# A vision-transformer block on one core: weight splits moved, high parts moved, and matmul groups at the norms

## The reference

```
h   = layernorm_3840(patches of x and of its four shifts) * gamma + beta, @ W + b   # tokens
h   = concat(cls, h)
y   = layernorm(h)
q, k, v = y @ Wq.T + bq, y @ Wk.T + bk, y @ Wv.T + bv          # 12 heads of 16
h   = h + softmax(q k.T / 4 + mask) v @ Wo.T + bo
z   = layernorm(h)
g   = top-2 gates of softmax(z @ router)                        # 8 experts of 192
routed = sum_e g_e * ((silu(z @ Wg_e) * (z @ Wu_e)) @ Wd_e)
shared = (silu(z @ Ws_gate) * (z @ Ws_up)) @ Ws_down            # 768 hidden
a   = sigmoid(z @ sg_w + sg_b)
out = h + a * shared + (1 - a) * routed
```

## Time and profile before

| | |
|---|---|
| median of 3 runs | 176.16 us (175.26 to 177.87) |
| profiled execution | 175.75 us, of which the span is 173.9 |
| granted TensorE clock, mean | 0.938 of 2.4 GHz |
| PE busy | 139.3 us, 80% |
| DVE busy | 120.5 us, 69% |
| ACT busy | 91.0 us, 52% |
| POOL busy | 42.1 us, 24% |

### The profile page before, as it was taken

One profiled execution on the slowest core, in us unless ns is written; L12 is line 12 of the kernel. 1 busy time (PEld: TensorE's weight loads), 2 busy tenths in 40 slices (PEclk: granted clock), 3 DMA queues, 4 the chain that ended last, 5 costly groups with the idle time before them and its releaser, 6 DMA issues.

```text
span 173.9 us, 4192 instructions
## 1 busy us (share of the span) xinstructions
PE 139.3 (80%) x1673; PEld 111.0 (64%) x1673; DVE 120.5 (69%) x297; ACT 91.0 (52%) x198; POOL 42.1 (24%) x55
## 2 busy tenths in 40 slices
PE   0449999903399988769806999999899999999992
PEld 0218777802177977659704567888777778878782
DVE  6299854699899996994626479787596562542753
ACT  0588865941277924444265769445645534343340
POOL 0000010000000000000000035536846858668430
PEclk9999999995579999999995589999999999999998
DMA  5999997000000000004991000048300000000003
GB/s 160 386 368 364 327 263 305 0 0 0 0 0 0 4 4 4 4 4 135 402 410 53 0 0 4 0 113 331 123 0 4 0 0 4 4 0 0 4 0 105
DMA packets 7391, 16.89 MB, mean 97 GB/s; under 512 B 800, under 2 KB 3612, under 8 KB 7372
## 3 DMA queue, kind: packets, MB, share of 16 engines
q1 hardware_dynamic: 7012, 16.29, 26.9%
q10 hardware_dynamic: 360, 0.34, 0.7%
HBM read 16.15 MB, written 0.47 MB: 96 GB/s over the span
## 4 chain that ended last, share of the span: by engine, by line
PE 50%; DVE 24%; ACT 9%; issue 5%; DMA 5%; ACTq 3%; POOL 2%; SPq 1%; DVEq 0%; POOLq 0%
PE PS L566 19%; PE PS L594 10%; PE PS L403 5%; DMA stage<-in_f_d_dram 5%; DVE piece L959 3%; DVE xsq L1115 3%; DVE mx L1111 2%; PE PS L322 2%; PE PS L415 2%; DVE vhl L1256 2%; PE PS L343 2%; PE PS L345 2%; PE PS L346 2%; PE PS L309 2%; POOL vhl L850 1%
## 5 line engine op out<-in xcount | busy, mean ns | idle before, releaser
L859 POOL TENSOR_TENSOR kq<-vhl,kq 128x296 f16<-128x296 f32 x35 | 29.5, 843 | 96.3 <-ACT kq L811 96.1
L1256 DVE SCALAR_TENSOR_TENSOR vhl<-PS,vhl 128x296 f32<-128x296 f32 x36 | 16.8, 466 | 21.6 <-POOL vhl L850 12.1
L804 ACT ACTIVATE vhl<-PS 128x296 f32<-128x296 f32 x36 | 15.0, 416 | 27.5 <-PE PS L566 27.5
L811 ACT ACTIVATE kq<-vhl 128x296 f16<-128x296 f32 x36 | 16.0, 445 | 5.5 <-DVE vhl L1256 5.5
L375 PE MATMUL PS<-cst,hn 128*128 128x128 f32 x10 | 4.0, 401 | 13.4 <-DVE hn L1035 13.4
L850 POOL TENSOR_TENSOR vhl<-vhl,xs 128x296 f32<-128x296 f32 x14 | 12.6, 903 | 5.5 <-issue 4.8
L1245 DVE TENSOR_TENSOR vhl<-vhl,xs 64x296 f32<-64x296 f32 (+1 forms) x18 | 10.2, 566 | 2.8 <-ACT vhl L804 2.6
L566 PE MATMUL PS<-XAh,piece 128*128 128x296 f16 x48 | 11.1, 316 | 0.2 <-DVE vhl L1256 0.2
L375 PEld LDWEIGHTS PS<-cst,hn 128*128 128x128 f32 x10 | 2.0, 201 | 14.0 <-DVE hn L1035 14.0
L566 PE MATMUL PS<-XAh,slab 128*128 128x296 f16 x48 | 10.0, 290 | 0.9 <-DVE vhl L1256 0.9
L343 PE MATMUL PS<-whl,xhl 128*128 128x193 f16 (+1 forms) x40 | 10.5, 262 | 0.0
(11 more groups left out here) (215 smaller groups left out, 403.0 us busy)
## 6 DMA issues: line engine op xcount, KB each, us to landing
slab<-in_w_inner_dram SPq DMA_DIRECT2D x3, 960.0 KB, 9.5
xs<-gate_rows_dram SPq DMA_DIRECT2D x8, 296.0 KB, 5.8
xs<-in_x_inner_dram SPq DMA_DIRECT2D x3, 592.0 KB, 10.5
stage<-in_f_a_dram SPq DMA_DIRECT2D x2, 768.0 KB, 10.4
stage<-in_f_b_dram SPq DMA_DIRECT2D x2, 768.0 KB, 11.7
stage<-in_f_d_dram SPq DMA_DIRECT2D x2, 576.0 KB, 13.2
xhl<-in_f_a_dram SPq DMA_DIRECT2D x1, 768.0 KB, 8.4
xhl<-in_f_b_dram SPq DMA_DIRECT2D x1, 768.0 KB, 9.3
```

Source lines behind the costliest of these rows:

```text
L804: A(silu[:, i % 2, :], PS[:, 3 + 2 * (i % 2), 0:HALF], ACT.Silu, scale=1.0 / XW).then_inc(S["a_silu"], 1)
L811: A(ah[:, f % ABUF, half * HALF:(half + 1) * HALF], hf[:, i % 3, :], ACT.Copy).then_inc(S["a_ah"], 1)
L859: G.tensor_tensor(al[:, f % ABUF, cols], hf[:, i % 3, :], ah[:, f % ABUF, cols], ALU.subtract).then_inc(S["g_al"], 1)
L1256: V.scalar_tensor_tensor(out=hf[:, i % 3, :], in0=PS[:, 4 + 2 * (i % 2), 0:HALF], scalar=SH / XW, in1=src[:, i % 2, :], op0=ALU.mult, op1= ...
```

## The change

Three kinds of edit, in the order of the engines:

- TensorE gets groups of matmuls of 512 columns whose results nobody reads, into bank 1 (free once the sums of squares have been read) and bank 6 (free between the attention and the second block half). At the first norm: 8 after `v_stat` has reached 5, 6 after the first three `h1` tiles, 6 after `v_stat` 10 and 4 after `v_stat` 11 (the reciprocal of `rsqrt(1)`). At the second: 6 right behind `wo(4)`, 4 after the last `h2` tile, 4 after `v_stat` 20 and 3 after `v_stat` 21.
- ScalarE converts WAh, WB and WC behind `squares(3)`, ahead of the bias rows, `sqrows` and `csum`. The second piece's first two high parts leave the place ahead of `root(3)`; all six stand at the steps 2 to 7 of the feed-forward, one a step (before: two ahead of the root and four at steps 2 to 5).
- VectorE makes the three low parts of the query and key weights ahead of the mean of the patches' norm, no longer behind `normed(0, range(3))`.

```diff
@@ tensor, ahead of transposes(0, ...)
+            def keep_warm(bank, n):
+
+                for _ in range(n):
+                    mm(PS[:, bank, :], WAh[:, 0:P], WAh[:, 0:512], start=True, stop=True)
+
+            pe.wait_ge(S["a_aw"], 1)
+            for name, count, n in (("v_stat", 5, 8), ("v_h", TILES + 3, 6), ("v_stat", 10, 6), ("v_stat", 11, 4)):
+                pe.wait_ge(S[name], count)
+                keep_warm(1, n)
@@ tensor, behind the output projection
             wo(4)
 
+            keep_warm(6, 6)
+            for name, count, n in (("v_h", 3 * TILES, 4), ("v_stat", 20, 4), ("v_stat", 21, 3)):
+                pe.wait_ge(S[name], count)
+                keep_warm(6, n)
             transposes(1, (0, 1, 2), range(TILES))
@@ scalar, behind the pixels
             squares(3)
 
+            act.wait_ge(d_aw, 80)
+            A(WAh[:, :], awst[:, 0, :], ACT.Copy, scale=SW).then_inc(S["a_aw"], 1)
+            A(WB[:, :], awst[:, 1, :], ACT.Copy, scale=SW).then_inc(S["a_aw"], 1)
+            A(WC[:, :], awst[0:CROWS, 2, :], ACT.Copy, scale=SW).then_inc(S["a_aw"], 1)
+
             act.wait_ge(S["p_bw"], 1)
...
             A(sqrows[:, 0:N].rearrange("p (a n) -> p a n", a=2), PS[:, 6:8, 0:HALF], ACT.Copy).then_inc(S["a_sqr"], 1)
-            act.wait_ge(d_aw, 80)
-            A(WAh[:, :], awst[:, 0, :], ACT.Copy, scale=SW).then_inc(S["a_aw"], 1)
-            A(WB[:, :], awst[:, 1, :], ACT.Copy, scale=SW).then_inc(S["a_aw"], 1)
-            A(WC[:, :], awst[0:CROWS, 2, :], ACT.Copy, scale=SW).then_inc(S["a_aw"], 1)
             act.wait_ge(S["p_main"], 1)
@@ scalar, second norm
             ctx_high(3)
-            ffn_high(1, 0)
-            ffn_high(1, 1)
             root(3)
@@ scalar, feed-forward loop
                     act_high(i - 1)
-                if 2 <= i < 6:
-                    ffn_high(1, i)
+                if 2 <= i < 8:
+                    ffn_high(1, i - 2)
@@ vector, ahead of the statistics
+            for k in range(3):
+                attention_low(k, 0, VC)
+
             stat = [0]
@@ vector, first norm
             normed(0, range(3))
-            attention_low(0, 0, VC)
-            attention_low(1, 0, VC)
-            attention_low(2, 0, VC)
             variances(2)
```

## The result

The changed kernel takes 173.96 us in the median of 20 runs (172.46 to 176.25), the kernel before 176.38 on the same chip (175.13 to 178.21); the ratio is 0.986, 95% interval 0.983 to 0.990. It is faster by 1.4%, clear of the interval but less than the 2% that the prediction took as telling: 2.4 us won where 5.2 were forecast (171.0, range 169.8 to 173.2), and the time lies outside the range. The profiled execution took 173.96, a span of 172.2.

The account below looks back on a forecast made before the run. VectorE paces the projections and TensorE the last stage, so only start time at the two norms could be won: 1.48 + 0.51 + 3.05 + 0.24 - 0.33 = 4.95 off 175.75 gives 170.8, taken as 171.0, range 169.8 to 173.2.

Parts of the forecast that it names:

- Part 1: First norm: VectorE's three low parts moved ahead of the statistics fill its idle time; gain 1.48 us, bounds 0.8 and 1.48.
- the first norm's clock: Matmul groups keep full clock there; earlier products and two closed VectorE gaps in the projections gain 0.51 us, bounds 0 to 0.75.
- The conversions and `csum`: First norm, ScalarE: weight conversions push `csum` to 32.9 at worst, before VectorE asks at about 34.8; cost nothing.
- Part 2: Second norm: moving two high parts from ahead of the root brings the reciprocal earlier; gain 3.05 us, lower bound 1.77.
- the table load: Second norm, ScalarE: goes right behind the last context copy, some 2 us before the variances; 1.28 us if left behind the wait.
- The gate's wait: Feed-forward step 6: a high part ahead of the gates' copy makes TensorE stand 0.33 us, bounds 0 and 0.6.
- Part 3: Matmul groups in TensorE's pauses at both norms hold the clock: gains 0.51 and 0.24 us, bounds 0 and 0.75 for both.
- the second norm's clock: Groups there spare ScalarE's XAh its wait for cold transposes: gain 0.24 us.
- Rival (a): Clock falls all the same around the norms' transposes, losing 0.51 + 0.24 and up to 0.7: 171.8 to 172.5; chance 0.12.
- Rival (c): Groups at both norms run at half clock ahead of the transposes, 3.9 and 3.6 us late: 179.2; chance 0.05.
- Rival (b): Feed-forward gives back more: a second stall like the gate's, table load left behind its wait: 172.6; chance 0.10.

Follow-up runs that it names:

- e1: Changed kernel without any of the matmul groups, moved splits and high parts kept: 177.53 us, ratio to before 1.008.
- e8: Changed kernel with ten matmuls in the attention's pause but no groups at the two norms: 175.46 us, ratio to before 0.997.
- e2: Kernel before with the norms' matmul groups alone added: 177.71 us.
- e7: e3 with the second piece's last two high parts at steps 7 and 8, behind the gates' copy: 170.54 us, ratio to before 0.971.
- e3: Changed kernel with ten more matmuls of 512 columns in the attention's pause ahead of the fourth unit's transposes: 171.85 us, ratio to before 0.977.
- e5: e3 with the second piece's first two high parts put back ahead of the second norm's root: 174.81 us, ratio to before 0.995.
- e11: e5 without the attention's ten matmuls: 173.99 us, ratio to before 0.986.
- e4: e3 with four matmuls instead of ten in the attention's pause: four runs, 171.01, 171.43, 174.70 and 174.82 us.
- e6: e3 with the attention weights' splits put back on ScalarE and VectorE: 173.28 us, ratio to before 0.989.

## Why the prediction was wrong

**Part 1** was right as a sum with the first norm's clock: 1.48 + 0.51 = 1.99 forecast, 1.96 measured to the maxima (1.55 to XAl and 0.41 behind it, so that the agreement to 0.03 is in part luck: one of the two gaps that the 0.51 is made of stayed). As terms they don't stand alone: the moved splits without groups gave 0.40 and 0.49 (e1, e8), the groups without moved splits were 1.32 slower in the profile of e2 (35.11 for 33.79). The splits bring the second matmuls forward, and with the clock down (from about 37.5 to 51 in e1, 40.7 to 51 in e8) TensorE then gives most of that back; the groups held it where no pause of 3.4 us followed them. The conversions and `csum` cost nothing; the weights landed at 26.1.

**Part 2** was right at its place: 3.05 forecast, 3.05 in the profiles (4.04 to 0.99), the table load where it was said to go. The gate's wait, 0.33 forecast, is 0.36 (e7). But the 3.05 are a gain only where the attention is on time (e3 against e5, 3.0 in the runs); where it is late by as much they are 0 (the changed kernel against e11).

**Part 3**: no group delayed a transpose, the second norm's clock gave 0.51 instead of 0.24. The step that failed is one that the prediction did not cost: it gave the clock back at the two norms and put the attention between them at no change, without a reason; the profile of before showed 1.00 there, for one execution. Rival (a), a fall around the norms' transposes, had the mechanism, at another place than the one that cost the time; at its own place the fall came in one profile only (e7, 1.0 us). Its reason against, that no gap left is as long as those in which the clock fell before, is what the runs refute: the clock fell 0.8 us after a pause of 2.65 us, 0.2 after one of 1.69 (e4), and in the midst of small matmuls (e1). That cost 3.02 us in the profile, and with it 170.9 became 173.96. With it put right (e3) the kernel took 171.85 in the median, its profiled execution 170.29.

Why the changed kernel falls in the attention in every profile and, by the mean clocks, probably in every execution, and the kernel before in a part of them, stays open. The moves alone bring the fall (e1), and so do the groups alone in the profile of e2, so neither of them is the one cause. In both profiles TensorE's work there is the same; the standing is not spread alike (the kernel before stands 0.88 between two score matmuls and 1.59 ahead of the transposes, the changed one 2.65 in one piece), but e1 fell with the former pattern. That the fall depends on when the stage comes is a guess that no run here tested.

**Rival (c)**, groups at half clock ahead of the transposes, is not seen at either norm in any profile; its mechanism is seen in the attention, where the ten matmuls added there came after a fall (e6, e8). Rival (b) did not come: the feed-forward lost only the gate's 0.4.

## What to carry to other kernels

A profile that shows full clock in a lightly loaded stage shows it for one execution: look at the mean clock of all of them, and price a fall there before counting on time won elsewhere. A wait that a change removes may have been covering another stage's variation, so cost its removal with that stage late as well as on time. Matmuls that hold the clock pay where no hole follows them; placed ahead of one they went with a fall at a worse moment (e2, e6), and once the clock has fallen they hold up the work behind them (e8).

## What the runs showed of the hardware

- The clock fell from 2.4 to 1.2 GHz while TensorE was busy with fp32 transposes and small products of 37 and 51 columns, with 0.57 us of standing shortly before (e1), which I had not expected. The Trainium skill says that a transpose does not count as busy for the gate (TensorE: Matmul & The Clock Gate, Part 4: PE-mode transpose). The fall in e1 would fit that; but the kernel before ran the same transposes and products at full clock in its profile (74.19 to 76.3), the transposes of the first norm kept full clock in the changed kernel, and no run here parts the transposes from the small products.
- A fall in the attention cost 1.5 us (e8, half clock from about 74.8 to 78.2, the delay by the group included), 3.0 (the changed kernel, 77.5 to 84.4) and 4.6 (e4, 76.2 to 86.4), in a stage of 25.7. One behind the second norm's transposes (96.7 to 100.1) cost nothing (e4).
- A matmul of 512 fp16 columns with its own weights took 0.225 to 0.235 us at full clock.
